# Two-layer graph kernel: one-hot comparisons of unequal width, two input loads on another queue, one GpSimd subtraction placed later

## What is computed

```python
deg = maximum(segment_sum(1, dst), 1); norm = deg ** -0.5
h = maximum(layernorm(x), 0)
for W_r, W_sl, W_el in two layers:                     # message layers
    self_msg = where(in_degree == 0, h @ W_el, h @ W_sl)
    agg = segment_sum((rel_embed[rel] + h[src]) @ W_r, dst)
    h = rrelu(agg * norm + self_msg)
x = x + h
h = maximum(layernorm(x), 0)
qk, v = h @ Wqk + bqk, h @ Wv + bv                     # attention over the same edges
attn = softmax over the edges of each dst of clip(qk[dst] . qk[src] / sqrt(128), -5, 5)
x = x + layernorm((segment_sum(attn * v[src], dst) @ Wo + bo) + h) * gamma + beta
```

## Time and profile before

| | before |
|---|---|
| median of 3 runs | 776.05 us |
| the profiled execution, its own time | 776.97 us |
| its span, first to last instruction | 775.2 us |
| granted TensorE clock, mean | 0.989 |
| busy: TensorE matmul / VectorE / ScalarE / GpSimd | 718.0 / 513.9 / 432.8 / 279.3 us |
| VectorE, line 870 (lo), 60 instructions | 114.4 us |
| VectorE, line 876 (m and r), 120 instructions | 126.6 us |

### The profile page before, as it was taken

The page is one execution under the profiler, slowest core; times in us unless marked ns, Lnnn a source line. Parts: engine busy times, 40 slices in busy tenths (PEclk is TensorE's granted clock), DMA queues, the critical chain, the costliest instruction groups (busy, mean ns, idle before and its releaser), DMA issues.

```text
span 775.2 us, 15480 instructions
## 1 busy us (share of the span) xinstructions
PE 718.0 (93%) x5805; PEld 534.4 (69%) x5805; DVE 513.9 (66%) x906; ACT 432.8 (56%) x1096; POOL 279.3 (36%) x293
## 2 busy tenths in 40 slices
PE   4686789999999999999999999799999999999996
PEld 2565788999899999889889998244444444444456
DVE  5999999988888877333234334245675757576676
ACT  1577566666666666641211223377676767767663
POOL 7299200000001222100000000366675757666664
PEclk9999999999999999999999999799999999999998
DMA  4101000133300000102231112110000100000010
GB/s 132 50 24 45 18 2 9 50 105 65 106 24 8 9 8 9 67 20 81 85 99 39 36 35 61 63 30 0 4 24 1 27 1 14 13 15 13 2 26 21
DMA packets 39763, 27.89 MB, mean 36 GB/s; under 512 B 5311, under 2 KB 38288, under 8 KB 39686
## 3 DMA queue, kind: packets, MB, share of 16 engines
q1 hardware_dynamic: 38514, 25.89, 11.5%
q10 hardware_dynamic: 1172, 0.98, 0.4%
HBM read 13.28 MB, written 10.80 MB: 31 GB/s over the span
## 4 chain that ended last, share of the span: by engine, by line
PE 71%; DMA 8%; DVE 8%; issue 5%; ACT 5%; SPq 2%; ACTq 1%; POOL 1%; POOLq 0%; DVEq 0%
PE sums L1568 17%; PE sums L1551 16%; PE sums L1047 12%; PE sums L1122 9%; PE sums L1086 8%; DVE work L876 3%; DMA x_after_messages<-work 2%; DMA h_attention<-work 2%; DMA work<-in_x 2%; SPq L580 2%; PE sums L1054 1%; DMA counts<-in_x 1%; DVE work L870 1%; ACT counts L1335 1%; PE sums L1061 1%
## 5 line engine op out<-in xcount | busy, mean ns | idle before, releaser
L1647 POOL TENSOR_TENSOR counts<-counts,work 125x500 f32<-125x500 f32 x150 | 165.0, 1100 | 100.0 <-DVE work L1717 94.7
L1717 DVE SCALAR_TENSOR_TENSOR work<-sums,counts 125x500 f32<-125x500 f32 x150 | 101.5, 677 | 106.1 <-ACT sums L1671 100.7
L1086 PE MATMUL sums<-work 125*128 125x196 f16 (+15 forms) x1220 | 153.7, 253 | 17.9 <-DVE work L876 17.9
L1568 PE MATMUL sums<-work 125*128 125x500 f32 (+1 forms) x350 | 159.7, 546 | 6.8 <-DVE work L1717 6.2
L1551 PE MATMUL sums<-work 128*125 128x500 f32 x300 | 152.2, 589 | 0.0
L1666 ACT ACTIVATE sums<-sums,steady 125x500 f32<-125x500 f32 (+1 forms) x157 | 102.0, 650 | 75.0 <-PE sums L1551 71.8
L1335 ACT CAST counts<-sums 128x364 f32 (+38 forms) x305 | 131.6, 473 | 2.3 <-issue 1.1
L870 DVE TENSOR_TENSOR work<-work,counts 125x3024 f16<-125x3024 f16 (+1 forms) x60 | 114.4, 1906 | 25.9 <-PE sums L1088 25.3
L1088 PE MATMUL sums<-work 125*128 125x10 f16 (+15 forms) x800 | 131.5, 194 | 0.0
L876 DVE TENSOR_TENSOR work<-work,counts 125x4200 f16<-125x4200 f16 (+15 forms) x120 | 126.6, 1093 | 0.0
L1047 PE MATMUL sums<-counts 125*128 125x250 f16 (+1 forms) x975 | 119.6, 266 | 3.7 <-ACT work L1263 3.5
(11 more groups left out here) (184 smaller groups left out, 734.8 us busy)
## 6 DMA issues: line engine op xcount, KB each, us to landing
first_columns<-counts SPq DMA_DIRECT2D x5, 610.4 KB
counts<-first_columns SPq DMA_DIRECT2D x5, 610.4 KB
counts<-counts SPq DMA_DIRECT2D x5, 468.8 KB
counts<-in_x SPq DMA_DIRECT2D x5, 312.5 KB
h_nodes<-counts SPq DMA_DIRECT2D x5, 312.5 KB
work<-in_x SPq DMA_DIRECT2D x12, 125.0 KB
x_after_messages<-work SPq DMA_DIRECT2D x12, 125.0 KB
h_attention<-work SPq DMA_DIRECT2D x12, 125.0 KB
```

Source lines behind the costliest of these rows:

```text
L1086: pe.matmul(win[:, 0:c, cols], lo[:, k * 2 * LO:k * 2 * LO + 128], m[:, k, h0 * w:(h0 + c) * w].rearrange("p (h d) -> p h d", d=w), start= ...
L1568: last = pe.matmul(ps_o[c % 2][:, 0:cols(u) // n], h3[:, source(c, j + i), :], pbuf[u % PB][:, i * NP:i * NP + cols(u) // n], start=j + i ...
L1647: pool.tensor_tensor(a, a, p, ALU.add).then_inc(acc_done, 1)
L1717: dve.scalar_tensor_tensor(pbuf[u % PB], ps_s[u % 4][0:NP, 0:WIDE], float(np.exp(-CLIP)), counts[0:NP, source(c, j), target(c) * WIDE:(tar ...
```

## The change

`lo` is no longer one array with 2 x 126 columns for a tile. It is an array of 126 columns for each tile (key 0) and, behind it, one of 100 columns for each tile (key 2), made by two comparisons, and line 1088 takes its 128 weight columns from the second. Since 28 more columns than a relation one-hot has are read, these weights hold columns of the next tile, or of `m` behind the last; the rows of the result that they make are not used. The batches' places in memory stay. Of the five loads of x, numbers 3 and 4 are issued by ScalarE, after its first small copy and ahead of the copies of the keys. GpSimd waits for `words_done`, and not only for dst, before lines 713 and 714, and its later wait for `words_done` is gone.

```diff
@@ ring
-    lo = view(work, at, NP, tiles * 2 * LO + 2, F16)
-    at += tiles * 2 * LO * 2
+    lo = view(work, at, NP, tiles * (LO + RL) + 28, F16)
+    at += tiles * (LO + RL) * 2
@@ SyncE
-            for i in range(5):
+            for i in range(3):
                 sp.dma_start(xs[:, 5 * i:5 * i + 5, :], x.rearrange("(j p) f -> p j f", p=NP)[:, 5 * i:5 * i + 5, :]).then_inc(x_in, 16)
@@ GpSimd
-            pool.wait_ge(edges_in[0], 16)
+            pool.wait_ge(words_done, 1)
             pool.tensor_copy(final, dst_i[:, EDGES - 1:]).then_inc(outside_set, 1)
             pool.tensor_tensor(steps_i[:, 1:], dst_i[:, :-1], dst_i[:, 1:], ALU.subtract).then_inc(outside_set, 1)
...
-
-            pool.wait_ge(words_done, 1)
             pool.wait_ge(outside_set, 5)
@@ VectorE
-                dve.tensor_tensor(lo[:, 0:t * 2 * LO].rearrange("p (t c two) -> p t c two", c=LO // 2, two=2),
-                                  iota_h[:, None, 0:LO].rearrange("p o (c two) -> p o c two", two=2).broadcast_to([NP, 2 * t, LO // 2, 2]),
-                                  key_lo.rearrange("p t (k two) -> p (t k) two", two=2)[:, :, None, :].broadcast_to([NP, 2 * t, LO // 2, 2]), ALU.is_equal)
+                for k, c0, c in ((0, 0, LO), (1, t * LO, RL)):
+                    dve.tensor_tensor(lo[:, c0:c0 + t * c].rearrange("p (t c two) -> p t c two", c=c // 2, two=2),
+                                      iota_h[:, None, 0:c].rearrange("p o (c two) -> p o c two", two=2).broadcast_to([NP, t, c // 2, 2]),
+                                      key_lo[:, :, None, 2 * k:2 * k + 2].broadcast_to([NP, t, c // 2, 2]), ALU.is_equal)
@@ TensorE
-                            pe.matmul(win[:, 0:c, cols], lo[:, k * 2 * LO:k * 2 * LO + 128],
+                            pe.matmul(win[:, 0:c, cols], lo[:, k * LO:k * LO + 128],
                                       m[:, k, h0 * w:(h0 + c) * w].rearrange("p (h d) -> p h d", d=w), start=t == 0, stop=False, skip_group_check=True)
-                        last = pe.matmul(win[:, c:, cols], lo[:, (2 * k + 1) * LO:(2 * k + 1) * LO + 128],
+                        last = pe.matmul(win[:, c:, cols], lo[:, n * GT * LO + k * RL:n * GT * LO + k * RL + 128],
@@ ScalarE
             act.copy(woken, zeros[0:1, 0:1]).then_inc(first_keys, 1)
+            for i in range(3, 5):
+                act.dma_start(xs[:, 5 * i:5 * i + 5, :], x.rearrange("(j p) f -> p j f", p=NP)[:, 5 * i:5 * i + 5, :]).then_inc(x_in, 16)
             for i, k in enumerate(KEY_ORDER):
```

## The result

The changed kernel took 772.86 us (median of 20 runs, 770.16 to 775.47) and the kernel before 775.00 us (median of 20 runs) beside it. The ratio is 0.9975, 95% interval 0.9964 to 0.9986: 0.25% faster by the ratio, 2.1 us by the medians (1.1 to 2.8 us by the interval). The forecast was 2.1 us less (773.9 against 776.05). The size came out; how it is made up did not. The ratios leave out the few runs in a slower state, here the one of 790.38 us of the kernel before.

The account below looks back on a forecast made before the run. VectorE was taken as the counting stage's bound to about batch 21, then TensorE. Parts 1, 2 and 3 summed as 2.1 + 0 + 0 us, median 776.05 to 773.9; own range 773.3 to 774.5, wider range 771.9 to 775.5.

Parts of the forecast that it names:

- What bounds the kernel: Counting stage: VectorE is the bound up to about batch 21, TensorE from there on; VectorE savings after that are worth nothing.
- Part 1: Narrower comparisons on VectorE: 0.15 us saved per 16-tile batch, 0.10 per 12-tile batch; 2.1 us comes through (1.8 to 2.5).
- that term: Batches 17 to 21, VectorE and TensorE nearly level: gain grows by 0.3 us, bounds 0 and 0.7.
- the places where the sum let savings go: Savings counted as lost in waits: batches 0 and 1 (0.30 us), 8 and 9 (0.3 us), 16, and after 21.
- The 0.59 us wait for the store: VectorE's wait behind batch 9 for a store of h, claimed to swallow the 0.3 us of batches 8 and 9.
- Part 2: Two loads of x on ScalarE's queue: no added bandwidth, landing stays at 27.2 us, worth 0.
- the sentence on the relation embeddings: Bound on x landing: up to 1.1 us later if relation embeddings and weights get in front of x's end.
- rival A: Loads of x: x lands earlier, VectorE goes on 1.5 us earlier; 772.4 us, at best 771.4; chance 0.17.
- Part 3: GpSimd's subtraction behind the words: words 1.28 us earlier, comparisons 0.9 to 2.64 us longer, hidden by the x wait; worth 0.
- Rival B: The saving doesn't come through: the store and GpSimd's chain after group 41 don't move with VectorE; 775.0 us, chance 0.12.
- I count 0: ScalarE's wait for GpSimd after group 41 grows from 0.3 to up to 1.3 us, against 2.35 us TensorE idles; no cost.
- Rivals A and C: C, beside rival A: ScalarE held in its two x issues, slower beyond 21.7 us; 779.3 us if until 25; chance 0.09.

## Why the prediction was right, and where it was not

**What bounds the kernel** held. The stretch from batch 23 to Wqk took 226.2 to 226.5 us in all 14 profiles, whatever VectorE did in it, and the narrower comparisons from batch 22 on gave nothing.

**Part 1** had the right prices. An added instruction and 416 columns less gave 0.15 us for each batch: batches 2 to 8 took 18.29 us instead of 19.17, 0.88 for six. All 21 batches of the stretch together are worth 18 x 0.15 + 3 x 0.10 = 3.0 us. (Of batches 17 to 21 three are long and two short, so all of that term is 0.65 us and not the 0.7 of the forecast's bound.) What failed are the places where the sum let savings go. The 0.59 us wait for the store was no fixed date: it comes and goes with the store's own time. One of the 13 other profiles had it again (0.6 us, the comparisons with the subtraction), the others 0.3 us or nothing. In the changed kernel 3.0 + 0.59, less 0.70 of longer waits for TensorE (0.71, 0.44 and 0.34 us at batches 17, 21 and 23, against 0.20, 0.34 and 0.25), make 2.9; measured were 85.05 - 82.34 = 2.7. So at batch 17 a saving was lost, as forecast, and more than forecast; the size of that wait goes with TensorE's clock (last section). With the comparisons alone VectorE did not wait there at all, and the stretch was 3.7 us shorter.

How far the sum was too small is not settled. The profile of before is the slowest of the five with the old comparisons up to batch 21: the other four took 83.89, 83.89, 83.93 and 84.27 us. Against these the changed kernel's 82.34 us are 1.5 to 1.9 us less, and the comparisons alone 2.6 to 3.0 us; the forecast's 2.1 lies between. That the gain is that of the comparisons is shown: 0.9951 with them alone, and no difference with either of the other parts alone.

**Part 2** failed at its value, and just beyond its bound. That a second queue brings no bandwidth held, also in its number: 100 GB/s at 0.37. But "the landing stays at 27.2" did not: it was 28.7 us, 1.5 us later, outside the 1.1 us that the sentence on the relation embeddings allowed for. That it is the move is shown by two kernels with it against eight without; its mechanism is open. The other reading of the even 101 GB/s, a load of 125 rows held by the few engines it gets, was put to the test with 120 rows: 208 GB/s at 0.92. That is where rival A's gain lay, not in the second queue.

**Part 3** was right in each step: line 811 at 0.16 us, a pair longer by 1.8 us (0.9 to 2.64 was forecast), VectorE ready at 25.40 (24.7 to 26.5), and nothing of it that the time can tell. One reading under it was off. The pair of comparisons at 68.69 us, taken as undisturbed (1.77 us), already lay beside one of GpSimd's casts; the pair of the same size at 110.34 us took 1.56. From 2.00 - 1.56 = 0.44 us for 256 columns, 999 columns come to 1.7 us; 1.8 were measured, where the forecast's lower end was 0.9.

**What hid the errors, and luck.** By the stages of the two profiles, the changed kernel won 2.7 us after batch 2, lost 1.5 us at x, and was 1.35 us ahead at Wqk, where the forecast had 2.1 and 0. In the median it is 2.1 us (1.1 to 2.8 by the interval), which agrees with 1.35 as well as with 2.1. So the hit is in part luck: a gain above the sum in one profile, a loss at x that the sum had at nothing, and a spread of runs wide enough to cover both.

**Rival B** was the one to take more seriously, and the sentence that let it go, "I count 0", is the weakest of the prediction. It took GpSimd's chain to start and to run as before. Its start did, its length did not: where they were left in their place, the 12 selects took 18.96 us in all five kernels with the old comparisons beside them, and 11.51 (three) or 29.4 to 29.9 us (three) with the narrower ones. With 18.96 ScalarE waits for the check 0.3 or 3.3 us, with 11.51 not at all, with 29.4 about 8 us. The changed kernel's profile had the short form. The code does not decide between them: up to batch 21 the kernel with only the narrower comparisons (11.51) and the one with them up to batch 21 (29.86) run the same comparisons. The changed kernel's 20 runs, 770.2 to 775.5, show none as late as the latest of two kernels whose profile had the long form (782.0 and 781.6); the runs of the third end at 774.3. Whether the changed kernel can fall into it isn't shown. In the three kernels with the selects moved, one profile each, ScalarE did not wait for the check.

**Rivals A and C.** x did not land earlier, and ScalarE was held only to 9.74 us.

## What to carry to other kernels

Before a saving is counted as lost behind a wait, ask whether that wait is a fixed date or a slow transfer that comes and goes; a second profile of the same code tells. Compare with more than one profile of the kernel before, too: here its only one was 0.8 to 1.2 us slower in the stage of interest than four kernels with the same code there. When an engine is made faster, look at the engines that run beside it: GpSimd's small instructions became longer or shorter by a factor here, and a check that was waited for 0.3 us was waited for 8 us in three kernels. Put such work where the busy engine idles anyway, as here the selects beside the wait for x. And a load held at an even, low rate with few of the DMA engines busy asks for another shape (120 rows and 5), not for another queue.

## What the runs showed of the hardware

- **GpSimd held off by VectorE for many instructions.** The cast of 100 x 256 took 0.40 us in the undisturbed case and 30.95 us beside back-to-back comparisons; 12 selects took 8.94 us beside batches 0 and 1 and the statistics, 18.96 us beside the old comparisons and 11.51 or 29.43 us beside the narrower ones; what decides between the last two is open. The Trainium skill (SBUF — State Buffer, Terms) has it that the loser of the shared port pair blocks fully for an instruction. The 30.95 us agree with the blocking, but they span the comparisons of seven batches and not one instruction. VectorE itself paid 1.9 us in all for the six instructions of the relations in the changed kernel (2.75 for 2.10 us at 62.18, 1.99 for 1.35 at 64.85, and 0.64 more at 67.50).
- **TensorE at half its clock, also where the profile lists full.** In five of the 14 profiles the granted clock fell from 1.00 to 0.50 (1.2 GHz) at 7.5 to 8.4 us, after TensorE had idled since 4.6 to 5.0 us, and was back for good at 93 to 97 us. Stretches of 20 us after:

```profile
60.00:80.00 20.00, 14.20 (x167) 12.26 (x166) 19.87 (x23) 15.48 (x58) 8.91 (x10) 0.50 0.14 38
80.00:100.00 20.00, 16.52 (x183) 14.71 (x182) 19.29 (x25) 11.95 (x40) 2.35 (x2) 0.68 0.07 18
100.00:120.00 20.00, 18.16 (x245) 16.51 (x242) 19.22 (x24) 13.55 (x43) 0.00 (x0) 1.00 0.01 2
```

  The other nine idled as long and list 1.00 there. But the same matmul lasts as long in them as at 0.50. First the changed kernel, listed at 0.50; then the kernel before, listed at 1.00 from its start on; then the kernel before again, a few us later:

```profile
90.23 0.33 PE L1086 MATMUL sums<-work 125*128 125x175 f16 x1
```

```profile
91.28 0.33 PE L1086 MATMUL sums<-work 125*128 125x175 f16 x1
...
96.96 0.25 PE L1086 MATMUL sums<-work 125*128 125x175 f16 x1
```

  In the nine, the first change of level that the trace records at all is a return to 1.00, at 75.1 to 95.9 us. In all 14 profiles these matmuls take 0.33 us in the median ahead of the first recorded return or where 0.50 is recorded, and 0.25 us where the record says that the full level is back. So in the nine the low level is very probably there and its record missing, and neither the 1.00 of rows 4 before 96 us nor the mean clock of 0.989 of before counts it. The kernel with only the subtraction (listed at 0.50) and the one with only the loads of x (listed at 1.00) took 83.89 and 83.93 us from batch 2 to batch 23: that pair says nothing of what the low level costs. What it costs can be seen at batch 17. In the eight profiles where the full level is back for good 1.1 us or more before batch 17 starts, VectorE does not wait for TensorE there; in four where it is back 0.6 to 0.8 us before, it waits 0.20 to 0.40 us; in two where it comes only afterwards, one of them the changed kernel, 0.71 us. Apart from the stall at batch 13, VectorE waits for TensorE nowhere else from batch 2 to batch 20 in any of the 14, so there the low level costs nothing. Compare the length of one matmul before you believe a clock column.
- **Layer 2 is uneven by itself.** The stretch from Wqk to Wv took 153.5 to 157.8 us in 14 profiles; that difference of 4.3 us is more than the whole gain of this change.
